# Scores and values of two steps at once in a windowed-attention kernel, with PSUM banks laid out anew

## The chip, the cores and the metric

The kernel runs on one core of a Trainium2 chip. The metric is device time in microseconds (us) for one execution of the whole program. Engines: PE is TensorE's matrix multiplication, PEld its weight load, DVE is VectorE, ACT is ScalarE, POOL is GpSimd, SP issues the transfers.

## The reference, cut to what matters

First comes a selective state-space block (about the first 365 us of the profile, untouched by this change apart from one mask tile). Then come six transformer layers on a batch of 2 sequences of 1,024 rows of width 128, all in fp32. In each layer, 16 heads of 64, windows of 32:

```python
qkv = x @ Wqkv;  q, k, v = split(qkv)
q = rotary(l2norm(q) * qs) * scale;  k = rotary(l2norm(k) * ks) / scale
sim  = einsum('bhwie,bhwje->bhwij', q, look_back(k)) * 8    # 32 queries by 64 keys
attn = softmax(where(mask, -big, sim))
out  = einsum('bhwij,bhwje->bhwie', attn, look_back(v))     # then out @ Wo
# then a layer norm and a gated feed-forward, a * gelu(gate) @ W2
```

## The kernel before

The attention is cut into 384 steps. A step is one pair of heads on 256 rows, 8 windows. A phase is 32 steps: one layer for one sequence, pairs outside, four pieces of rows inside. There are 12 phases. The part of the previous phase that follows the attention (output projection, norm, feed-forward) is threaded into the steps of the phase that runs, at the step numbers `u = n % 32` that the constants `U_WO` (output projection, two halves), `U_MEAN`, `U_DEV`, `U_VAR`, `U_INV`, `U_Z` and `U_FFN` name.

Step `m` is software-pipelined over loop turns `n`. Each engine runs an order written out by hand, once a turn, and semaphores tie the engines together: `then_inc` on the instruction that produces, `wait_ge` ahead of the one that needs. The count a wait asks for is the number of steps that must have got so far. What happens to step `m`:

| work | engine | turn before | semaphore |
|---|---|---|---|
| project q, k (banks 0, 1) and v (bank 5, upper half) | PE L1033, L1040 | m | qk_ps, v_ps |
| squares, and v copied to SBUF | ACT L1266, L1285 | m | sq, v_cp |
| sums of squares (`norms`) | DVE L1385 | m | ss |
| rotary products (`tables`), read from banks 0, 1 | DVE L1404, L1406 | m+1 | prods |
| inverse norms, of two steps at once (`norm_pair`) | ACT L1220, L1223 | every second turn | rn |
| rotary sums, scaling | POOL L1505 to L1510 | m+2 | qk |
| transpose q, k (bank 2), copy | PE L1019, ACT L1259 | m+4 | qkT |
| mask products, scores (banks 3, 4) | PE L975, L981 | m+5 | s_ps |
| row minimum (`least`), exponents | DVE L1361, ACT L1233 | m+5 | mn, pr |
| transpose exponents (bank 6), copy | PE L1054, ACT L1275 | m+6 | pT |
| values (banks 5, 6), reciprocal and scaling (`normalise`) | PE L1000, DVE L1373, L1376 | m+7 | o_ps, on |
| transpose the output (bank 3), copy to OT | PE L958, ACT L1248 | m+8 | oT |

Scores and values use the array in tiles of 64 rows by 32 columns; one step has 32 of each product. All else on PE uses the whole 128 by 128. In fp32 each product of the code is two instructions in the profile. A bank of PSUM that one engine writes is not read by another at the same time: several waits exist only for that, such as the one of the v projection for `on`.

## Time and profile before

| | |
|---|---|
| runs | 2062.97, 2067.97, 2070.41 us; median 2067.97 |
| the profiled execution | 2066.36 us |
| its span in the trace | 2064.6 us (1.8 us lie around it) |
| busy, share of the span | PE 96%, DVE 74%, ACT 67%, POOL 59% |
| mean granted clock of TensorE | 0.978 of full |

Busy time counts an instruction from its start to its end. Neighbours on one engine overlap: a PE product is in flight for some 0.2 us after the next has begun. So what one costs is the distance from its start to the next one's start, and the durations add up to more than that.

### The profile page before, as it was taken

How to read it: one execution, taken by the hardware profiler on the slowest of the kernel's cores; microseconds unless marked ns; L12 is line 12 of the kernel's file. 1: busy time of each engine (PE TensorE's matmuls, PEld its weight loads, DVE VectorE, ACT ScalarE, POOL GpSimd, SP SyncE). 2: the span in 40 equal slices, each digit the busy share in tenths (PEclk: the TensorE clock that was granted, in tenths of full speed). 3: DMA queues.
4: the chain of work that ended last, by engine and by line, in shares of the span. 5: the costliest groups of instructions: out<-in, count | busy, mean ns of one | idle time of the engine just before them, and what ended most of it. 6: DMA issues, size and time to landing. Idle time of an engine off the chain costs nothing.

```text
span 2064.6 us, 82312 instructions
## 1 busy us (share of the span) xinstructions
PE 1989.6 (96%) x33044; PEld 1399.8 (68%) x33044; DVE 1518.1 (74%) x2875; ACT 1383.4 (67%) x4164; POOL 1225.6 (59%) x1374
## 2 busy tenths in 40 slices
PE   7789798999999999999999999999999999999998
PEld 3333233887686786876876877868768778687684
DVE  1499897886796776867867967769678678686783
ACT  4533233886786777767867867768678677776783
POOL 1376774775584565765746855648557567565570
PEclk9888989999999999999999999999999999999999
DMA  1321110311131111121211311112211111111110
GB/s 62 134 72 70 63 61 0 105 44 38 39 90 42 40 43 39 45 77 36 53 37 37 96 38 41 44 32 50 76 47 43 40 39 49 38 43 33 24 40 22
DMA packets 148091, 104.30 MB, mean 51 GB/s; under 512 B 15778, under 2 KB 140256, under 8 KB 146176
## 3 DMA queue, kind: packets, MB, share of 16 engines
q1 hardware_dynamic: 147712, 99.07, 17.3%
q8 instruction: 259, 4.24, 0.9%
q14 instruction: 120, 0.98, 0.1%
HBM read 48.31 MB, written 1.18 MB: 24 GB/s over the span
## 4 chain that ended last, share of the span: by engine, by line
PE 82%; issue 0%; POOL 0%; ACT 0%; DVE 0%; POOLq 0%; ACTq 0%
PE ps L1033 20%; PE ps L1040 9%; PE ps L1019 8%; PE ps L1058 8%; PE ps L1000 8%; PE ps L981 7%; PE ps L1054 4%; PE ps L958 4%; PE ps L1098 3%; PE ps L1092 3%; PE ps L1103 3%; PE ps L975 2%; PE ps L1078 1%; PE ps L1087 1%; PE ps L1133 0%
## 5 line engine op out<-in xcount | busy, mean ns | idle before, releaser
L1510 POOL TENSOR_TENSOR QK<-QK,RN 128x512 f32<-128x512 f32 x384 | 400.8, 1044 | 374.2 <-ACT RN L1223 359.1
L1233 ACT ACTIVATE PR<-ps,MN 128x64 f32<-128x64 f32 x1536 | 357.3, 316 | 154.6 <-DVE MN L1361 139.8
L1033 PE MATMUL ps<-W,XS 128*128 128x256 f32 x1536 | 435.3, 406 | 4.9 <-PEq L64 4.1
L1505 POOL TENSOR_TENSOR QK<-PC,PS 128x256 f32<-128x256 f32 x384 | 280.7, 731 | 246.4 <-PE ps L1019 243.7
L1259 ACT COPY QKT<-ps 128x512 f32<-128x512 f32 x384 | 225.0, 586 | 248.6 <-PE ps L1019 248.6
L1385 DVE TENSOR_REDUCE SS<-SQ 128x8 f32<-128x512 f32 x384 | 262.3, 683 | 58.0 <-ACT SQ L1266 55.2
L1033 PEld LDWEIGHTS ps<-W,XS 128*128 128x128 f32 x1536 | 261.0, 189 | 61.5 <-issue 4.9
L1506 POOL TENSOR_TENSOR QK<-PC,PS 128x256 f32<-128x256 f32 x384 | 281.3, 733 | 0.0
L1361 DVE TENSOR_REDUCE MN<-ps 128x4 f32<-128x256 f32 x384 | 163.0, 424 | 149.8 <-PE ps L981 148.5
L1404 DVE TENSOR_TENSOR PC<-ps,TC 128x512 f32<-128x512 f32 x384 | 261.4, 681 | 0.1
L1406 DVE TENSOR_TENSOR PS<-ps,TS 128x512 f32<-128x512 f32 x384 | 260.7, 679 | 0.0
L1266 ACT ACTIVATE SQ<-ps 128x512 f32<-128x512 f32 x384 | 244.2, 636 | 3.7 <-PE ps L1033 3.7
L1040 PEld LDWEIGHTS ps<-W,XS 128*128 128x128 f32 x1536 | 213.4, 190 | 49.1 <-DVE ON L1376 20.6
L1040 PE MATMUL ps<-W,XS 128*128 128x128 f32 x1536 | 240.2, 279 | 1.2 <-issue 1.2
L1019 PE MATMUL ps<-ident,QK 128*128 128x128 f32 x1536 | 233.8, 273 | 0.9 <-POOL QK L1510 0.6
L1000 PE MATMUL ps<-V,PT 64*32 64x65 f32 x12288 | 227.2, 226 | 0.2
L1019 PEld LDWEIGHTS ps<-ident,QK 128*128 128x128 f32 x1536 | 182.7, 141 | 45.7 <-issue 42.5
L716 POOL TENSOR_TENSOR scr<-U,scr 128x1024 f32<-128x1024 f32 x64 | 150.7, 2355 | 80.8 <-DVE scr L599 80.6
L1000 PEld LDWEIGHTS ps<-V,PT 64*32 64x32 f32 x12288 | 190.6, 105 | 0.9 <-issue 0.8
L484 ACT ACTIVATE ps<-DL,a_neg 128x1024 f32<-128x1024 f32 x64 | 71.6, 1118 | 169.0 <-DVE scr L599 167.7
L981 PE MATMUL ps<-QKT 64*32 64x64 f32 x12288 | 174.5, 222 | 0.0
L1376 DVE TENSOR_TENSOR ON<-ps,RC 128x256 f32<-128x256 f32 x384 | 162.9, 424 | 13.6 <-DVE RC L1373 0.5
(142 smaller groups left out, 3226.7 us busy)
## 6 DMA issues: line engine op xcount, KB each, us to landing
V<-V SPq DMA_DIRECT2D x384, 97.5 KB, 2.2
scr<-B_rows SPq DMA_DIRECT2D x32, 512.0 KB, 3.5
V<-V SPq DMA_DIRECT2D x288, 32.5 KB, 2.4
W<-in_Wqkv SPq DMA_DIRECT2D x40, 192.0 KB, 2.8
TC<-in_tcos SPq DMA_DIRECT2D x6, 1024.0 KB, 5.9
TS<-in_tsin SPq DMA_DIRECT2D x6, 1024.0 KB, 8.5
WO<-in_Wo SPq DMA_DIRECT2D x6, 512.0 KB, 4.1
W<-in_W SPq DMA_DIRECT2D x6, 341.0 KB
```

The costliest lines, as they stand in the source:

```text
L981: mm = nc.tensor.matmul(ps[32 * quad:32 * quad + 32, 3 + h, slot * DH:(slot + 1) * DH], QKT[DH * h:DH * h + DH, 0, c0:c0 + WIN], QKT[DH * ...
L1000: mm = nc.tensor.matmul(ps[32 * quad:32 * quad + 32, 5 + slot, h * (DH + 1):(h + 1) * (DH + 1)], PT[r, m % 2, h, 32 * quad:32 * quad + 32] ...
L1019: mm = nc.tensor.transpose(ps[:, 2, (x * 2 + k) * P:(x * 2 + k + 1) * P], src, ident[:])
L1033: mm = nc.tensor.matmul(ps[:, par, k * 2 * P:(k + 1) * 2 * P], cols[k], W[:, i, 0:2, :].rearrange("p t m -> p (t m)"), start=True, stop=True)
L1040: mm = nc.tensor.matmul(ps[:, 5, (2 + k) * P:(3 + k) * P], cols[k], W[:, i, 2, :], start=True, stop=True)
L1233: e = nc.scalar.activation(PR[:, m % 2, h, slot * DH:(slot + 1) * DH], ps[:, 3 + h, slot * DH:(slot + 1) * DH], ACT.Exp, scale=-1.0, bias= ...
L1385: nc.vector.tensor_reduce(SS[:, p % 2, 8 * k:8 * k + 8], SQ[:, n % 2, :, :], AX.X, ALU.add).then_inc(ss, 1)
L1404: nc.vector.tensor_tensor(PC[:, par, :, :].rearrange("p (k a) d -> p k (a d)", k=2), src, TC[l % 2][:, 2 * s:2 * s + 2, :], ALU.mult)
L1406: nc.vector.tensor_tensor(PS[:, par, :, :].rearrange("p (k a) d -> p k (a d)", k=2), src, TS[l % 2][:, 2 * s:2 * s + 2, :], ALU.mult).then ...
L1505: nc.gpsimd.tensor_tensor(QK[:, par, :, 0:hd], PC[:, par, :, 0:hd], PS[:, par, :, hd:DH], ALU.add)
L1506: nc.gpsimd.tensor_tensor(QK[:, par, :, hd:DH], PC[:, par, :, hd:DH], PS[:, par, :, 0:hd], ALU.add).then_inc(rot, 1)
L1510: nc.gpsimd.tensor_tensor(QK[:, par, :, :], QK[:, par, :, :], bcast_last(RN[:, m // 2 % 2, 8 * par:8 * par + 8], DH), ALU.mult).then_inc(q ...
```

## The change

- **Scores and values.** In every even turn, PE makes the scores of steps n-6 and n-5 together, then the values of steps n-8 and n-7 together; in odd turns neither. A mask product now covers both steps (256 columns instead of 128, from a mask tile with three parts).
- **Row minimum and normalise** run in even turns only, once for two steps: one reduction of 512 elements a partition, one reciprocal of 8, two multiplications. On DVE they now come after `clamp_pair` and `tables`.
- **Banks.** Scores of two steps take the lower halves of banks 3 and 4. The v projection moves from bank 5 to the upper half of bank 4, the transposed output to the upper half of bank 3, the transposed exponents to the last quarters of banks 5 and 6.
- **Waits.** The v projection is now apart from that of q and k (`project_v`), and waits for `pr >= n - 5`: the exponents of the same turn. The second q, k product of an even turn waits for the minimum of the same turn. The transposes of q and k for an odd turn are made in the even turn before it, between the two projections. The exponents of an odd turn wait for the output transposes of that turn, whose second one waits for the v copy of the turn before.
- **ScalarE's order.** `copy_qk`, (`norm_pair` in even turns,) `exponents`, `copy_out`, `squares`, `copy_v`, `copy_p`.
- Later parts of the pipeline shift by a turn (exponents in m+6 or m+5, output transposes m+9), the threaded part by one turn (`U_FFN` 16 to 17), and the loop drains for 9 turns instead of 8.

```diff
-U_WO, U_MEAN, U_DEV, U_VAR, U_INV, U_Z, U_FFN, U_TAB = (6, 8), (7, 9), (8, 10), (10, 12), (11, 13), (12, 14), 16, 17
...
-                return 8 <= n < NSTEPS
+                return 10 <= n < NSTEPS
...
-                m = n - 8
+                m = n - 9
...
+                    if steady(n) and n % 2 == 1 and k == 1:
+                        pe.wait_ge(v_cp, n)
...
                     src = ON[:, m % 2, :, :].rearrange("p (k h) d -> p k (h d)", k=2)[:, k, :]
-                    mm = nc.tensor.transpose(ps[:, 3, (1 + k) * P:(2 + k) * P], src, ident[:])
+                    mm = nc.tensor.transpose(ps[:, 3, (2 + k) * P:(3 + k) * P], src, ident[:])
...
+                if n % 2 or not 0 <= n - 6 < NSTEPS:
+                    return
...
+                    if h == 0:
+                        pe.wait_ge(v_cp, min(n, NSTEPS))
                     if steady(n) and h == 1:
-                        pe.wait_ge(v_sh[(n - 7) % 4], 32 * ((n - 7) // 4 + 1))
-                    nc.tensor.matmul(ps[:, 3 + h, 0:P], identb[:], MASKB[:, int(s == 0), h, :], start=True, stop=True)
+                        pe.wait_ge(v_sh[(n - 8) % 4], 32 * ((n - 8) // 4 + 1))
+                    nc.tensor.matmul(ps[:, 3 + h, 0:2 * P].rearrange("p (f c) -> p f c", f=2), identb[:],
+                                     MASKB[:, f:f + 2, h, :], start=True, stop=True)
                 if steady(n):
...
+                    pe.wait_ge(v_sh[(n - 7) % 4], 32 * ((n - 7) // 4 + 1))
+                for m in (n - 6, n - 5):
+                    s = place(m)[3]
...
+                            mm = nc.tensor.matmul(ps[32 * quad:32 * quad + 32, 3 + h, o0:o0 + DH],
...
+                    mm.then_inc(s_ps, 1)
...
+                if n % 2 or not 0 <= n - 8 < NSTEPS:
                     return
...
+                    for m in (n - 8, n - 7):
...
+                pe.wait_ge(pT, n - 6)
+                for m in (n - 8, n - 7):
+                    for h in range(2):
+                        for slot, quad in spread_tiles:
+                            j = window(slot, quad)
+                            r = slice(64 * slot, 64 * slot + 64)
+                            o0 = (2 * (m % 2) + h) * (DH + 1)
+                            mm = nc.tensor.matmul(ps[32 * quad:32 * quad + 32, 5 + slot, o0:o0 + DH + 1],
...
+                                                  V[r, 2 * (m % 8) + j // 4, 2 * (1 - j % 2) + h, :], start=True, stop=True)
+                    mm.then_inc(o_ps, 1)
...
+                if not steady(n) or n % 2:
                     wait(pe, qkT, m)
                 pe.wait_ge(qk, m + 1)
...
+                        if steady(n) and n % 2 == 0 and (x, k) == (1, 0):
+                            pe.wait_ge(oT, n - 9)
                         src = QK[:, m % 2, :, :].rearrange("p (k x h) d -> p k x (h d)", k=2, x=2)[:, k, x, :]
                         mm = nc.tensor.transpose(ps[:, 2, (x * 2 + k) * P:(x * 2 + k + 1) * P], src, ident[:])
                 mm.then_inc(qkT_ps, 1)
...
                 wait(pe, prods, n - 1)
                 cols = [XS[:, b, PAD + s * STEP + k * P:PAD + s * STEP + (k + 1) * P] for k in range(2)]
                 for k in range(2):
+                    if k == 1 and n % 2 == 0:
+                        wait(pe, mn, n - 4)
                     mm = nc.tensor.matmul(ps[:, par, k * 2 * P:(k + 1) * 2 * P], cols[k],
                                           W[:, i, 0:2, :].rearrange("p t m -> p (t m)"), start=True, stop=True)
                 mm.then_inc(qk_ps, 1)
+
+            def project_v(n):
+                if n >= NSTEPS:
+                    return
...
-                wait(pe, on, n - 6)
+                wait(pe, pr, n - 5)
                 for k in range(2):
-                    mm = nc.tensor.matmul(ps[:, 5, (2 + k) * P:(3 + k) * P], cols[k], W[:, i, 2, :], start=True, stop=True)
+                    if steady(n) and n % 2 == 1 and k == 1:
+                        pe.wait_ge(pT, n - 6)
+                    mm = nc.tensor.matmul(ps[:, 4, (2 + k) * P:(3 + k) * P], cols[k], W[:, i, 2, :], start=True, stop=True)
                 mm.then_inc(v_ps, 1)
...
+                wait(pe, on, min(n - 6 - n % 2, NSTEPS))
                 for h in range(2):
-                    if h == 1 and 7 <= n < NSTEPS - 1:
+                    if h == 1 and n % 2 and 7 <= n < NSTEPS - 1:
                         pe.wait_ge(qkT, n - 3)
-                    mm = nc.tensor.transpose(ps[:, 6, (2 + h) * P:(3 + h) * P], PR[:, m % 2, h, :], ident[:])
+                    if h == 1 and n % 2 == 0 and steady(n + 1):
+                        pe.wait_ge(oT, n - 8)
+                    mm = nc.tensor.transpose(ps[:, 5 + h, 3 * P:4 * P], PR[:, m % 2, h, :], ident[:])
                 mm.then_inc(pT_ps, 1)
...
-                qk_transposed(n)
+                if n % 2 == 0:
+                    qk_transposed(n)
                 out_transposed(n)
                 scores(n)
                 values(n)
                 project(n)
+                if n % 2 == 0:
+                    qk_transposed(n + 1)
+                project_v(n)
                 p_transposed(n)
...
+                p = (n - 2) // 2
+                if n % 2 or not 0 <= p < NSTEPS // 2:
...
-                m = n - 5
+                m = n - 6
...
+                if m % 2:
+                    wait(act, oT_ps, min(n - 8, NSTEPS))
                 for h in range(2):
                     for slot in range(2):
+                        o0 = (m % 2) * P + slot * DH
...
+                                                 ps[:, 3 + h, o0:o0 + DH], ACT.Exp, scale=-1.0,
+                                                 bias=MN[:, h, 2 * (m % 2) + slot:2 * (m % 2) + slot + 1])
                 e.then_inc(pr, 1)
...
+                act.wait_ge(mn, min(n - 4 - n % 2, NSTEPS))
...
+                nc.scalar.copy(PT[:, m % 2, :, :], ps[:, 5:7, 3 * P:4 * P]).then_inc(pT, 1)
...
+                if n % 2 and n >= 9:
+                    act.wait_ge(v_sh[(n - 7) % 4], 32 * ((n - 7) // 4 + 1))
...
-                               ps[:, 5, 2 * P:4 * P].rearrange("p (k a d) -> p k a d", k=2, d=DH)).then_inc(v_cp, 1)
+                               ps[:, 4, 2 * P:4 * P].rearrange("p (k a d) -> p k a d", k=2, d=DH)).then_inc(v_cp, 1)
...
+                if n % 2 == 0:
+                    copy_qk(n)
+                    norm_pair(n)
+                    exponents(n)
+                    copy_out(n)
+                    squares(n)
+                    copy_v(n)
+                    copy_p(n)
+                else:
+                    copy_qk(n)
+                    exponents(n)
                 if u == U_FFN and t >= 0:
                     load_set(nc, act, GELU)
...
                     gates(t, (0,))
+                    copy_v(n)
+                    gates(t, (1,))
                     copy_p(n)
...
                     load_set(nc, act, EXP_LN)
-                else:
+                elif n % 2:
                     copy_out(n)
                     squares(n)
+                    copy_v(n)
                     copy_p(n)
-                    copy_v(n)
...
+                if n % 2 or not 0 <= n - 6 < NSTEPS:
+                    return
+                dve.wait_ge(s_ps, n - 4)
+                wait(dve, pr, n - 6)
+                nc.vector.tensor_reduce(MN[:], ps[:, 3:5, 0:2 * P].rearrange("p h (a d) -> p h a d", d=DH),
+                                        AX.X, ALU.min).then_inc(mn, 2)
...
+                p = (n - 8) // 2
+                if n % 2 or not 0 <= n - 8 < NSTEPS:
+                    return
+                dve.wait_ge(o_ps, 2 * p + 2)
+                o = ps[:, 5:7, 0:4 * (DH + 1)].rearrange("p s (q d) -> p s q d", q=4)
+                wait(dve, on, 2 * p)
+                nc.vector.reciprocal(RC[:].unsqueeze(3), o[:, :, :, DH:DH + 1]).then_inc(rc, 1)
+                dve.wait_ge(rc, p + 1)
+                for k in range(2):
+                    wait(dve, oT_ps, 2 * p + k - 1)
+                    nc.vector.tensor_tensor(ON[:, k, :, :].rearrange("p (s h) d -> p s h d", s=2),
+                                            o[:, :, 2 * k:2 * k + 2, 0:DH], bcast_last(RC[:, :, 2 * k:2 * k + 2], DH),
+                                            ALU.mult).then_inc(on, 1)
...
+                clamp_pair(n)
+                tables(n)
                 least(n)
                 normalise(n)
-                clamp_pair(n)
-                tables(n)
                 norms(n)
```

## Rows read from the trace of the kernel before

**Rows 1.** The page: busy times, and the chain that ended last, by engine.

```profile
PE 1989.6 (96%) x33044; PEld 1399.8 (68%) x33044; DVE 1518.1 (74%) x2875; ACT 1383.4 (67%) x4164; POOL 1225.6 (59%) x1374
...
PE 82%; issue 0%; POOL 0%; ACT 0%; DVE 0%; POOLq 0%; ACTq 0%
```

**Rows 2.** PE in order of start, one step; columns start, duration (both us), instruction.

```profile
1283.88 0.60 PE L1019 MATMUL ps<-ident,QK 128*128 128x128 f32 x4
...
1284.53 0.28 PE L975 MATMUL ps<-MASKB,identb 128*128 128x128 bf16 x2
...
1285.00 0.59 PE L1000 MATMUL ps<-V,PT 64*32 64x65 f32 x32
1285.53 1.13 PE L1033 MATMUL ps<-W,XS 128*128 128x256 f32 x4
1286.49 0.61 PE L1040 MATMUL ps<-W,XS 128*128 128x128 f32 x4
...
1287.16 0.60 PE L1019 MATMUL ps<-ident,QK 128*128 128x128 f32 x4
```

**Rows 3.** PE in narrow windows: where tiled products begin and end.

```profile
1212.82 0.22 PE L975 MATMUL ps<-MASKB,identb 128*128 128x128 bf16 x1
1212.97 0.29 PE L981 MATMUL ps<-QKT 64*32 64x64 f32 x8
...
1213.61 0.22 PE L1000 MATMUL ps<-V,PT 64*32 64x65 f32 x1
1213.76 0.48 PE L1033 MATMUL ps<-W,XS 128*128 128x256 f32 x1
...
1214.08 0.59 PE L1033 MATMUL ps<-W,XS 128*128 128x256 f32 x2
```

**Rows 4.** ACT in order of start, a stretch without gaps.

```profile
1220.07 0.38 ACT L1285 COPY V<-ps 128x256 f32<-128x256 f32 x1
1220.33 0.70 ACT L1295 ACTIVATE DEV<-ps,epsc 128x512 f32<-128x512 f32 x1
1221.06 0.63 ACT L1297 ACTIVATE DEV<-DEV 128x512 f32<-128x512 f32 x1
1221.60 0.57 ACT L1259 COPY QKT<-ps 128x512 f32<-128x512 f32 x1
1222.07 0.93 ACT L1233 ACTIVATE PR<-ps,MN 128x64 f32<-128x64 f32 x4
...
1223.12 0.64 ACT L1266 ACTIVATE SQ<-ps 128x512 f32<-128x512 f32 x1
```

**Rows 5.** DVE in order of start; x2 is two instructions.

```profile
1284.23 0.69 DVE L1385 TENSOR_REDUCE SS<-SQ 128x8 f32<-128x512 f32 x1
...
1286.28 0.68 DVE L1404 TENSOR_TENSOR PC<-ps,TC 128x512 f32<-128x512 f32 x1
1286.88 0.68 DVE L1406 TENSOR_TENSOR PS<-ps,TS 128x512 f32<-128x512 f32 x1
...
1208.04 1.39 DVE L1412 TENSOR_TENSOR XS<-XS,ps 64x512 f32<-64x512 f32 x2 [6.03 <-PE ps L1058]
```

**Rows 6.** What follows a release: four engines in order of start, idle before in brackets.

```profile
1212.75 0.59 ACT L1259 COPY QKT<-ps 128x512 f32<-128x512 f32 x1 [0.60 <-PE ps L1019]
...
1213.55 0.42 DVE L1361 TENSOR_REDUCE MN<-ps 128x4 f32<-128x256 f32 x1 [0.55 <-PE ps L981]
...
1214.17 0.42 DVE L1376 TENSOR_TENSOR ON<-ps,RC 128x256 f32<-128x256 f32 x1
...
1214.64 0.19 PEld L1040 LDWEIGHTS ps<-W,XS 128*128 128x128 f32 x1 [0.16 <-DVE ON L1376]
...
1214.73 0.30 PE L1040 MATMUL ps<-W,XS 128*128 128x128 f32 x1
```

**Rows 7.** Windows in the state-space part: span, busy by engine, granted clock, DMA.

```profile
228.50:259.20 30.70, 24.68 (x54) 9.17 (x53) 28.95 (x18) 9.22 (x9) 27.52 (x19) 1.00 0.18 68
259.20:262.60 3.40, 3.40 (x5) 1.33 (x4) 3.15 (x3) 0.87 (x2) 2.79 (x2) 0.50 0.01 2
```

More of the change, by code:

```diff
@@ L689, in _ @@
             pool.wait_ge(s_id, 1)
-            nc.gpsimd.tensor_copy(MASKB[:].rearrange("p f h c -> p (f h c)"), MASK).then_inc(s_half, 1)
-            nc.gpsimd.tensor_copy(identb[:], ident[:])
+            for f, first in enumerate((1, 0, 0)):
+                nc.gpsimd.tensor_copy(MASKB[:, f, :, :].rearrange("p h c -> p (h c)"), MASK[:, first * 2 * P:(first + 1) * 2 * P])
+            nc.gpsimd.tensor_copy(identb[:], ident[:]).then_inc(s_half, 1)
             pool.wait_ge(ld_qks, 16)
@@ L952, in out_transposed @@
                 if not steady(n):
-                    wait(pe, pr, min(n - 5, NSTEPS))
+                    wait(pe, pr, min(n - 6, NSTEPS))
+                    wait(pe, mn, min(n - 6 + n % 2, NSTEPS))
                     wait(pe, oT, m)
@@ L963, in scores @@
-                if not 0 <= m < NSTEPS:
+                if n % 2 or not 0 <= n - 6 < NSTEPS:
                     return
-                b, l, i, s, par = place(m)
-                if m == 0:
+                if n == 6:
                     pe.wait_ge(s_ones, 2)
                 if not steady(n):
-                    wait(pe, pr, m)
-                    wait(pe, oT, m - 3)
-                    pe.wait_ge(qkT, m + 1)
+                    wait(pe, pr, n - 6)
+                    wait(pe, oT, min(n - 9, NSTEPS))
+                    pe.wait_ge(qkT, n - 4)
@@ L985, in scores @@
-                mm.then_inc(s_ps, 1)
+                    pe.wait_ge(v_sh[(n - 7) % 4], 32 * ((n - 7) // 4 + 1))
+                for m in (n - 6, n - 5):
+                    s = place(m)[3]
+                    for slot in range(2):
+                        for h, quad in spread_tiles:
+                            c0 = PAD + s * STEP + window(slot, quad) * WIN
+                            o0 = (m % 2) * P + slot * DH
+                            mm = nc.tensor.matmul(ps[32 * quad:32 * quad + 32, 3 + h, o0:o0 + DH],
+                                                  QKT[DH * h:DH * h + DH, 0, c0:c0 + WIN],
+                                                  QKT[DH * h:DH * h + DH, 1, c0 - WIN:c0 + WIN],
+                                                  start=False, stop=True, skip_group_check=True)
+                    mm.then_inc(s_ps, 1)
@@ L987, in values @@
             def values(n):
-                m = n - 7
-                if not 0 <= m < NSTEPS:
+                if n % 2 or not 0 <= n - 8 < NSTEPS:
                     return
                 if not steady(n):
-                    pe.wait_ge(pT, m + 1)
-                    pe.wait_ge(v_sh[m % 4], 32 * (m // 4 + 1))
-                    wait(pe, on, m)
-                wait(pe, v_cp, min(n, NSTEPS))
-                for h in range(2):
-                    for slot, quad in spread_tiles:
-                        j = window(slot, quad)
-                        r = slice(64 * slot, 64 * slot + 64)
-                        mm = nc.tensor.matmul(ps[32 * quad:32 * quad + 32, 5 + slot, h * (DH + 1):(h + 1) * (DH + 1)],
-                                              PT[r, m % 2, h, 32 * quad:32 * quad + 32],
-                                              V[r, 2 * (m % 8) + j // 4, 2 * (1 - j % 2) + h, :], start=True, stop=True)
```

66 lines of the change are left out of this document (14 added, 52 removed).

## The prediction

> **What bounds the kernel now.** I read the page first. The chain that ended last is 82% PE, with nothing else above 0%, and PE is busy 96% of the span [rows 1]. So the question became what one step costs on PE and whether it ever waits. PE in order of start answers both [rows 2]: a step takes 1287.16 - 1283.88 = 3.28 us, start to start, without a gap. Most of the 384 steps repeat that number. Per turn, six transposes take 0.65, masks and scores 0.47 (1284.53 to 1285.00), values and the way to the projection 0.53, the q, k projection 0.96, then v projection and two transposes 0.67. Anything that PE does less pays in full, and any new wait of PE costs in full. ScalarE is busy 67% of the span, VectorE 74% [rows 1]; neither sets the pace. Of ScalarE's spacings (start to start, without gaps) [rows 4] gives 0.26 for the copy of v (I take the same for the exponents' copy, of as many elements), 0.47 for the q, k copy, 0.93 from the first exponent to the end of the fourth, 1.05 from the first exponent to the squares.
>
> **What it removes.** PE changes between full and tiled products twice a step. The last mask starts at 1212.82, the first score at 1212.97: 0.15 instead of 0.06. The last value starts at 1213.61, the first projection at 1213.76: 0.15, where its neighbours follow at about 0.01. That first projection needs 0.32 (to 1214.08), where three more in 0.96 - 0.32 make 0.21 each [rows 2, 3]. So one round in and out costs 0.09 + 0.14 + 0.11 = 0.34. Between scores and values another 0.05 goes, an estimate. A pair of steps now has one round instead of two: 0.39 saved. The masks cost the same: two of 256 columns for four of 128 (bounded by 0.06 and 0.11 each; if a wide one cost as little as a narrow one, 0.1 more a pair). PE alone would need 6.56 - 0.39 = 6.17 a pair; times 192 pairs that is 75 us saved.
>
> **What it adds: the frame of a pair on PE**, in us from the first transpose of the even turn, if nothing waits. Output transposes 0.44, masks 0.65, scores 0.96, last score 1.46, values 1.49, last value 2.20, q, k projection 2.35, its second product 2.88, transposes for the odd turn 3.32, v projection 3.75, its last product 4.08, exponent transposes 4.20. Odd turn: output transposes 4.41, q, k projection 4.63, v projection 5.50, exponent transposes 5.94, end 6.17.
>
> Latencies come from [rows 6]. ACT starts 0.31 after the start of PE's last product (one mask and three transposes back from 1212.82, at 0.06 and 0.11, the last q, k transpose starts at 1212.44, and its copy at 1212.75). DVE starts 0.35 after the last score (1213.20 by the 0.27 that scores take, to 1213.55). DVE's product ends at 1214.59, the weight load starts at 1214.64, PE's product at 1214.73: 0.14 from a release to PE. On one engine it is 0.03 (1221.03 to 1221.06) [rows 4].
>
> *Even turn.* The minimum starts at 1.46 + 0.35 = 1.81 if DVE is free. A reduction of 512 is 0.69 [rows 5]; least could cost 0.42, as 256 do now [rows 6], at most twice that, 0.85; I take 0.69. It ends at 2.50, PE may go on at 2.64, before 2.88. The exponents run from 2.53 to 3.46, and 3.60 is before 3.75. Reciprocal and products end by about 3.5, before 4.20; so does the output copy, by about 3.9. All this is covered, with 0.15 to 0.3 to spare.
>
> *Odd turn: here it breaks.* The v copy can't begin before 4.08 + 0.31 = 4.39. ScalarE then has the v copy (0.26), the exponents' copy (0.26), the q, k copy (0.47), and only then the odd step's exponents (0.93), which end at 6.31. `project_v` of the odd turn waits for them, since it writes the bank that they read: 6.31 + 0.14 = 6.45, where PE is ready at 5.50. That is a stall of 0.95 in every pair. Nothing can be in front of it: PE's whole odd projection is already over. Behind the waiting product are queued the exponent transposes and the next pair's scores. The wait for the v copy at the odd output transpose lies inside the same chain (4.39 + 0.38 + 0.14 = 4.91 against 4.52) and costs nothing more.
>
> The row's order on ScalarE is what counts here. The profile shows its instructions only ever in program order. 
> A second chain closes over DVE: odd exponents, 1.05 to the squares, 0.64 for them, 0.03, the sum (0.69), 0.03 and the clamp (0.10, estimated), rotary products 1.20, minimum 0.69, 0.03, exponents 0.93, 0.14, four v products 0.33 to the last, 0.31, copies 0.26 + 0.26 + 0.47: 7.16 a pair. The first gives 6.17 + 0.95 = 7.12. They are as good as equal; I take 7.13, so +0.57 for a pair.
>
> **Pairs with threaded work** (u = 8 to 19), each against before:
> - (8,9), (10,11): the mean's product (2 x 0.43) comes between v_ps and the odd projection and covers 0.86 of 0.95. But the two additions after the output projection (1.39 [rows 5]) now stand, with clamp and rotary products, before the minimum. They start about 0.2 into the turn (an estimate: the last product of the output projection is still in flight): 0.20 + 1.39 + 0.10 + 1.20 = 2.89, ends 3.58, PE goes on at 3.72 instead of 2.88: 0.84, plus 0.07 for the exponents. Before, some 0.13 was lost. Together -0.39 + 0.10 + 0.91 - 0.13 = +0.5 each.
> - (12,13), (14,15): the two activations of the inverse deviation (1220.33 to 1221.60, 1.27 [rows 4]) now end an even row, inside the chain: +0.57 + 1.27, less 0.1 lost before: +1.7 each.
> - (18,19): the additions of the feed-forward (estimated at 1.5 on DVE, by the 1.39 of [rows 5]) stand before the minimum like those above: +0.57 + 1.0 - 0.3 = +1.3.
> - Pair (16,17) holds the feed-forward: its own chain is unchanged, +0.57.
>
> A phase: 11 x 0.57 + 2 x 0.5 + 2 x 1.7 + 1.3 = 12.0. Eleven phases 132, the first (no threaded work) 9, one more turn of draining 1: +142. From the profiled 2066.4 that is 2208; that execution stands 1.6 under the median of the runs, which is less than their spread. I say 2205.
>
> **Bounds.** Low: latencies and overlaps better by 0.1 in each chain (-19), the inverse hidden (-28), minimum 0.42: 2150. High: minimum 0.85, which lengthens the second chain by 0.16 (+31), 0.1 more of latency (+19): 2260. POOL, busy 59% [rows 1], is no bound: its input is ready a turn before its result is needed.
>
> **The rivals.**
> 1. *The saving comes through, faster.* ScalarE's row hides in its own idle time and PE doesn't stand at `project_v`. This decides if the stretch from v_ps to the odd exponents' end is at most 1.42 + 0.39 = 1.81 (equal) or 1.42 (all saved), where I add 0.31 + 0.26 + 0.26 + 0.47 + 0.93 + 0.14 = 2.37. For it: ScalarE is busy 67% of the span and has time to spare [rows 1]. Against it: each term is a row. Time 2066 - 75 = 1991, about 2000 with the stalls of u = 8 to 19.
> 2. *The clock.* TensorE is granted 1.00 (2.4 GHz) all through the attention. It would now be idle nearly 1 us of every 7. In the state-space part, PE busy 24.7 of 30.7 us at 1.00 was followed by 3.4 us at 0.50 (1.2 GHz) [rows 7]. If that came here once in 34 us, each would cost some 1.1 us (half of 3.4, for the two thirds of the pair that PE sets): 48 x 1.1 = 54, so 2260; as often as once in 14 us, 2340. Against it: idle here is 13%, there 20%.
> 3. *DVE becomes the bound* through a wide minimum near 0.85: 2236, within my range.
>
> **Chances.** Forecast with its bounds (rival 3 in it) 0.79; rival 2 0.12; rival 1 0.06; a stall of just about what is saved, 0.03. The range 2145 to 2265 takes in the bounds and the mild end of rival 2. A measurement here can't tell less than 0.3% (6 us) from no change: faster 0.07, same 0.02, slower 0.91.
>
> **What would show it.** Right: PE's biggest idle is before `project_v`, released by ACT's exponents, 0.9 to 1.0 us long, once a pair; score starts 7.1 apart; L1033's first product slow once a pair; a second idle of about 0.8 at u = 8, 10, 18 released by the minimum; 1.2 more at u = 13, 15. Wrong: no idle before `project_v` and 6.2 a pair (rival 1), stretches at 0.50 after 400 us (rival 2), a minimum over 0.8 (rival 3), or a saving that is not 0.39.

## The result, and the profile after

The changed kernel takes 2281.93 us (median of three, 2276.24 to 2282.14) against 2067.97: 1.103 times as long, 95% interval 1.0989 to 1.1072. The forecast was 2205 (2145 to 2265): the direction was right, the time 77 us too short. The profiled execution has a span of 2280.1 us against 2064.6.

From the page, by engine: busy times, the chain that ended last, and two of the costliest groups (busy, mean ns | idle before).

```profile
PE 2034.3 (89%) x32660; PEld 1359.1 (60%) x32660; DVE 1460.2 (64%) x2491; ACT 1426.2 (63%) x4164; POOL 1238.2 (54%) x1376
...
PE 62%; ACT 12%; issue 7%; DVE 3%; ACTq 0%; DVEq 0%
...
L1058 PE MATMUL ps<-W,XS 128*128 128x128 f32 x1536 | 259.3, 291 | 102.1 <-ACT PR L1260 98.3
...
L1010 PE MATMUL ps<-V,PT 64*32 64x65 f32 x12288 | 184.4, 228 | 8.2 <-issue 8.2
```

The chain was 82% PE, with nothing else above 0% [rows 1]. Now it goes through ScalarE for 12%, and 98.3 us of PE's idle time stand before the v projection, released by the exponents: the stall that was forecast, where it was forecast. One ordinary pair on PE, in order of start:

```profile
1445.58 0.60 PE L1027 MATMUL ps<-ident,QK 128*128 128x128 f32 x4
...
1446.23 0.38 PE L980 MATMUL ps<-MASKB,identb 128*128 128x256 bf16 x2
1446.55 0.81 PE L990 MATMUL ps<-QKT 64*32 64x64 f32 x61
...
1448.06 1.13 PE L1043 MATMUL ps<-W,XS 128*128 128x256 f32 x4
1449.03 0.60 PE L1027 MATMUL ps<-ident,QK 128*128 128x128 f32 x4
1449.47 0.61 PE L1058 MATMUL ps<-W,XS 128*128 128x128 f32 x4
...
1450.13 0.74 PE L962 MATMUL ps<-ident,ON 128*128 128x128 f32 x2
1450.71 1.03 PE L1043 MATMUL ps<-W,XS 128*128 128x256 f32 x4
1452.13 0.71 PE L1058 MATMUL ps<-W,XS 128*128 128x128 f32 x4 [0.39 <-ACT PR L1260]
1452.68 0.38 PE L1074 MATMUL ps<-ident,PR 128*128 128x128 f32 x2
1452.89 0.59 PE L1078 MATMUL ps<-OT,WO 128*128 128x512 f32 x1
```

The pair takes 1452.89 - 1445.58 = 7.31, where [rows 2] give 6.56. ScalarE in the same stretch:

```profile
1450.11 0.38 ACT L1313 COPY V<-ps 128x256 f32<-128x256 f32 x1 [0.15 <-PE ps L1058]
1450.38 0.38 ACT L1301 COPY PT<-ps 128x256 f32<-128x256 f32 x1
1450.64 0.60 ACT L1285 COPY QKT<-ps 128x512 f32<-128x512 f32 x1
1451.12 0.95 ACT L1260 ACTIVATE PR<-ps,MN 128x64 f32<-128x64 f32 x4
```

Spacings 0.27, 0.26, 0.48, and the odd v projection 1.01 after the first exponent: the four links of the forecast's first chain, back to back. Its idle is printed as 0.39, not 0.95. Part of the delay is taken earlier: 0.36 at the second output transpose, which waits for the v copy (1450.13 to 1450.71 is 0.58, where the even turn has 0.22). Here it is 0.55: four q, k products that don't follow tiled ones need 0.87, so PE was ready at 1451.58. The printed idle begins only when the last of them is no longer in flight. 0.36 and 0.55 make 0.91, for 0.95 forecast.

Pair by pair (q, k projection to q, k projection, mean over phases 1 to 10), the difference to the kernel before, beside the forecast:

| pairs of a phase | before to after, each | difference | forecast |
|---|---|---|---|
| the eleven forecast at +0.57 | eight of them 6.57 to means of 7.31 to 7.55 (medians 7.30 to 7.34); (4,5) 6.80 to 8.12; (6,7) 14.50 to 14.19, (16,17) 23.70 to 24.15 | +7.8 | +6.3 |
| (8,9), (10,11) | 14.46 to 15.88, 7.48 to 10.12 | +4.1 | +1.0 |
| (12,13), (14,15) | 7.47 to 9.82, 6.92 to 8.55 | +4.0 | +3.4 |
| (18,19) | 6.57 to 8.80 | +2.2 | +1.3 |
| a phase | | +18.1 | +12.0 |

The first two rows are not like for like. The threaded work moved on by one turn, and with it a product for the mean (0.86) went from pair (6,7) to pair (10,11). The forecast left that out. It changes no sum, but with that product taken out of both pairs the first row is +8.7 and the second +3.2.

### The profile page after: what moved, and what is told of

Its sections match the earlier page's. It is cut to its first block, busy times and chain, and to the rows that moved or that the text cites. A ratio compares the mean times of both kernels' runs of the same rounds, so it can differ in the third digit from the quotient of the medians.

```text
span 2280.1 us, 80744 instructions
## 1 busy us (share of the span) xinstructions
PE 2034.3 (89%) x32660; PEld 1359.1 (60%) x32660; DVE 1460.2 (64%) x2491; ACT 1426.2 (63%) x4164; POOL 1238.2 (54%) x1376
## 3 DMA queue, kind: packets, MB, share of 16 engines
q8 instruction: 257, 4.21, 0.8%
## 4 chain that ended last, share of the span: by engine, by line
PE 62%; ACT 12%; issue 7%; DVE 3%; ACTq 0%; DVEq 0%
PE ps L1058 10%; PE ps L1043 9%; PE ps L1027 7%; PE ps L1078 7%; ACT PR L1260 7%; PE ps L990 6%; PE ps L1010 5%; PE ps L1118 3%; PE ps L1112 3%; PE ps L1123 3%; ACT PT L1301 3%; PE ps L1074 2%; PE ps L962 2%; PE ps L980 2%; ACT QKT L1285 2%
## 5 line engine op out<-in xcount | busy, mean ns | idle before, releaser
L1043 PE MATMUL ps<-W,XS 128*128 128x256 f32 x1536 | 427.8, 397 | 44.5 <-DVE MN L1396 37.2
L1058 PE MATMUL ps<-W,XS 128*128 128x128 f32 x1536 | 259.3, 291 | 102.1 <-ACT PR L1260 98.3
L1058 PEld LDWEIGHTS ps<-W,XS 128*128 128x128 f32 x1536 | 203.1, 192 | 180.6 <-ACT PR L1260 171.0
L1027 PEld LDWEIGHTS ps<-ident,QK 128*128 128x128 f32 x1536 | 189.1, 142 | 52.1 <-issue 32.4
L962 PE MATMUL ps<-ident,ON 128*128 128x128 f32 x768 | 183.7, 286 | 22.6
L1010 PE MATMUL ps<-V,PT 64*32 64x65 f32 x12288 | 184.4, 228 | 8.2 <-issue 8.2
L1078 PE MATMUL ps<-OT,WO 128*128 128x512 f32 x384 | 169.9, 593 | 0.0
L1313 ACT COPY V<-ps 128x256 f32<-128x256 f32 x384 | 143.7, 374 | 39.4 <-PE ps L1058 20.9
L990 PE MATMUL ps<-QKT 64*32 64x64 f32 x12288 | 165.2, 224 | 0.0
```

The lines of the kernel that those rows point to most:

```text
L990: mm = nc.tensor.matmul(ps[32 * quad:32 * quad + 32, 3 + h, o0:o0 + DH], QKT[DH * h:DH * h + DH, 0, c0:c0 + WIN], QKT[DH * h:DH * h + DH, ...
L1010: mm = nc.tensor.matmul(ps[32 * quad:32 * quad + 32, 5 + slot, o0:o0 + DH + 1], PT[r, m % 2, h, 32 * quad:32 * quad + 32], V[r, 2 * (m % 8 ...
L1027: mm = nc.tensor.transpose(ps[:, 2, (x * 2 + k) * P:(x * 2 + k + 1) * P], src, ident[:])
L1043: mm = nc.tensor.matmul(ps[:, par, k * 2 * P:(k + 1) * 2 * P], cols[k], W[:, i, 0:2, :].rearrange("p t m -> p (t m)"), start=True, stop=True)
L1058: mm = nc.tensor.matmul(ps[:, 4, (2 + k) * P:(3 + k) * P], cols[k], W[:, i, 2, :], start=True, stop=True)
L1078: mm = nc.tensor.matmul(ps[:, wo_bank(t, c), :], WO[:, k, :], OT[:, c, k, :], start=(k == 0), stop=(k == PAIRS - 1), skip_group_check=True)
```

## The experiments

All start from the changed kernel unless another is named. The ratio is to the kernel before, run on the same chip; "pair" is the median of the eight pairs of a phase without threaded work, phases 1 to 10.

| run | us | ratio (95%) | pair |
|---|---|---|---|
| e1_copy_in_chain | 2347.17 | 1.134 (1.131 to 1.137) | 7.62 |
| e2_copy_in_idle | 2279.79 | 1.102 (1.098 to 1.105) | 7.32 |
| e3_minimum_first | 2482.30 | 1.200 (1.197 to 1.203) | 8.64 |
| e4_exps_first_min_first | 2436.29 | 1.178 (1.175 to 1.182) | 8.38 |
| f5_clamp_min_first | 2242.07 | 1.084 (1.082 to 1.087) | 7.32 |
| f6_exps_first | 2285.97 | 1.105 (1.102 to 1.108) | 7.58 |
| f7_exps_and_min_first | 2214.78 | 1.071 (1.069 to 1.074) | 7.06 |
| f8_all_three | 2231.76 | 1.079 (1.078 to 1.081) | 7.31 |
| g1_inverse_odd | 2271.85 | 1.099 (1.097 to 1.101) | 7.31 |
| g2_inverse_odd_clamp_min | 2229.62 | 1.079 (1.077 to 1.081) | 7.32 |
| g3_three_edits | 2202.75 | 1.066 (1.064 to 1.069) | 7.07 |
| g4_both_exponents_even | 2141.24 | 1.036 (1.034 to 1.038) | 6.74 |
| h1_split_changed | 2318.35 | 1.121 (1.119 to 1.122) | 7.58 |
| h2_split_both_exponents | 2129.00 | 1.029 (1.026 to 1.032) | 6.74 |
| h3_var_later_both_exponents | 2124.63 | 1.028 (1.026 to 1.031) | 6.75 |
| h4_var_later_inverse_odd | 2251.47 | 1.088 (1.086 to 1.090) | 7.32 |

**Is it the chain through ScalarE?** One more copy (256 elements a partition, into a tile that nobody reads) in even rows, once inside the chain and once in ScalarE's idle time before the even exponents.

```diff
+            def extra():
+                nc.scalar.copy(JNK[:], XRES[:, 0:STEP])
...
                     copy_p(n)
+                    if 10 <= n < NSTEPS:
+                        extra()
```

In e2 the same two lines stand behind `norm_pair(n)` instead.

> The changed kernel with one more ScalarE copy (128x256, SBUF to SBUF, result unused) at the end of each even row from turn 10 on, that is between the exponents' copy and the odd row. Theory A (a chain from the even turn's v projection through ScalarE's copies and the odd exponents to the odd v projection sets the pair): the copy's 0.26 us comes on top in every one of some 187 pairs, +50 us, about 2332 us, and TensorE's wait before the odd v projection grows by 0.26. Theory B (a chain over VectorE's sums and minimum, or TensorE's own work, sets the pair, and the wait is slack): 0 to +10 us.

> The same extra copy, but after norm_pair in each even row, where ScalarE in the profile waits 1.0 us for the minimum. Theory A: nothing, 2282 us within 6 us. Theory C (ScalarE's total work sets the pair, wherever it stands): +50 us, as in the kernel with the copy in the chain.

The same work costs 65 us in one place and nothing (-2) in the other. Pair 7.62 against 7.32. What counts is the place in ScalarE's row and not its load: the chain is shown. (e1 came out 15 us above its forecast. Its pair grew by 0.30 instead of 0.26, some 7 us in 187 pairs, and its clock fell more often, which is told below and can hold the rest.)

**What may VectorE's order do?** The minimum ahead of clamp and rotary products; then behind the clamp only.

```diff
-                clamp_pair(n)
-                tables(n)
                 least(n)
                 normalise(n)
+                clamp_pair(n)
+                tables(n)
                 norms(n)
```

This is e3. In f5 `clamp_pair(n)` stays first and `tables(n)` alone moves.

> The changed kernel with VectorE's old order in even turns: least, normalise, clamp_pair, tables, norms. Theory A: the ordinary pair stays at 7.30 us (7.25 to 7.35), since the chain over ScalarE is untouched; the pairs at u = 8, 10 and 18, where TensorE now waits 1.1 us for a minimum that stands behind additions and rotary products, lose that wait: 3 x 1.1 x 11 = 36 us, about 2246 us. Theory B (the chain over VectorE sets the ordinary pair): the pair falls below 7.2 us, and the gain is over 50 us.

> As the kernel with the minimum first, which came out 200 us slower, but with the clamp kept ahead of it: clamp_pair, least, normalise, tables, norms. In that kernel ScalarE's norm_pair, which stands before the exponents in its row, waited 478 us in all for a clamp that had moved behind the minimum and normalise. If that was the cause, it is gone here: the ordinary pair is 7.30 us again (7.25 to 7.40), and the pairs at u = 8, 10 and 18 lose their wait for the minimum: 36 us, about 2246 us. If the order itself hurts (rotary products late), the ordinary pair is above 7.5.

e3 missed badly, on the other side of its forecast. Its chain of waits names the reason in one line (total us, times, longest):

```profile
ACT SS L1244 <- DVE SS L1427: 478.3, 192, 4.7
```

`norm_pair` stands ahead of the even exponents on ScalarE and needs the clamp; with the clamp behind the minimum and both products of `normalise`, every pair pays. In the changed kernel the same wait is 35.1 us in all. I had costed the wait that I removed and not the one that the moved instruction carries. f5 keeps the clamp in front and lands where forecast: 2242, with u = 8 from 15.9 to 14.7, u = 10 from 10.1 to 8.9, u = 18 from 8.8 to 7.6, and the ordinary pair unchanged. That is the second term of the forecast (the minimum late at u = 8, 10, 18), shown and worth 40 us.

**The chain without the q, k copy.** In odd rows the exponents come ahead of `copy_qk`; the wait for the v copy moves from the odd output transpose to the odd v projection, so that it doesn't close a circle.

```diff
                 else:
-                    copy_qk(n)
                     exponents(n)
+                    copy_qk(n)
...
-                    if steady(n) and n % 2 == 1 and k == 1:
-                        pe.wait_ge(v_cp, n)
...
+                if steady(n) and n % 2:
+                    pe.wait_ge(v_cp, n)
```

> The changed kernel, VectorE's order untouched; in odd rows the exponents go before the q, k copy, and the wait for the v copy moves from the second output transpose to the odd v projection. The chain over the copies gets 0.47 shorter, the one over VectorE (odd squares, sum, clamp, rotary products, minimum, exponents, v projection, v copy) stays as long as it is, 0.13 below the pair of now. With both chains real, the ordinary pair is 7.17 us and the time 2257 us (2245 to 2265). If VectorE's chain doesn't bind, 6.83 and 2194 us.

> As the kernel with the minimum first, and besides: in odd rows the exponents go before the q, k copy, and the wait for the v copy moves from the second output transpose to the odd v projection, so that the exponents need not wait for it. Theory A: the chain gets 0.47 us shorter and the ordinary pair 7.30 - 0.47 = 6.83 us; with the 36 us of the order, 2282 - 88 - 36 = 2160 us (2145 to 2185). Theory B: the squares of the odd step come 0.47 later, which lengthens the chain over VectorE unless its order is the old one, as here; then no more than the 36 us, 2246 us. A third possibility is that the rotary products, now late in even turns, make TensorE wait at the odd q, k projection: 6.9 to 7.1 us a pair.

> Both edits: exponents first in odd rows, and clamp, minimum, normalise ahead of the rotary products. Both chains are shorter: the ordinary pair 6.83 us, unless TensorE waits at the odd q, k projection for the rotary products that are now late (ready at about 5.2 us of the pair, where the projection is due at 4.6), which gives 6.85 to 6.95. Time 2246 - 88 = 2158 us (2145 to 2180). If neither chain is the cause, nothing beyond the 36 us.

Alone (f6) it gives nothing (2286 us, for 2257 forecast): the second chain, over VectorE, takes over. ScalarE and VectorE of f6:

```profile
1431.15 0.95 ACT L1260 ACTIVATE PR<-ps,MN 128x64 f32<-128x64 f32 x4
...
1438.57 0.94 ACT L1260 ACTIVATE PR<-ps,MN 128x64 f32<-128x64 f32 x4
```

```profile
1434.10 0.38 DVE L1427 TENSOR_SCALAR SS<-SS 128x16 f32<-128x16 f32 x1
1434.40 0.68 DVE L1439 TENSOR_TENSOR PC<-ps,TC 128x512 f32<-128x512 f32 x1
```

From odd exponents to odd exponents are 7.42, and each link of the second chain follows the one before it there. In the changed kernel the same circle is 7.18: it has only 0.13 of slack in 7.31, at the even v projection (exponents ready at 1448.27 + 0.93 + 0.14 = 1449.34, product at 1449.47). In f6 the clamp takes 0.30 of it where it took 0.08 (1446.27 to 1446.35), and no run tells why. e4, with e3's order, has e3's wait (479.0 us). With f5's order (f7) the median pair goes to 7.06 and the time to 2215, where 2158 was forecast. So two chains did stand side by side, and undoing one of them shows only the other. Of the 0.47 that leave the first, 0.26 arrive in the median pair; some pairs take 7.7, and the idle inside the values' products (below) grows from 8.2 to 27.3 us.

**The inverse deviation.**

```diff
-U_WO, U_MEAN, U_DEV, U_VAR, U_INV, U_Z, U_FFN, U_TAB = (7, 9), (8, 10), (9, 11), (11, 13), (12, 14), (13, 15), 17, 17
+U_WO, U_MEAN, U_DEV, U_VAR, U_INV, U_Z, U_FFN, U_TAB = (7, 9), (8, 10), (9, 11), (11, 13), (13, 15), (14, 16), 19, 17
```

> The changed kernel with one thing moved: the two activations of the inverse deviation stand in odd turns (u = 13, 15) instead of even ones (12, 14), the steps behind them one or two turns later. Theory A (the chain v projection, ScalarE's copies, odd exponents, odd v projection is what sets a pair; what stands at the end of ScalarE's even row is inside it, what ends the odd row is not): the pairs u = 12 and 14 lose 1.27 each, 11 phases x 2 x 1.27 = 28 us, so 2254. Rival B (ScalarE's work as a sum sets the pair, wherever it stands): no change, 2282.

> The inverse deviation in odd turns as in the run before it, together with VectorE's order clamp, minimum, normalise, tables (that alone gave 2242). Theory A: the two gains touch different pairs' stalls and add up: 2242 - 28 = 2214. Rival B: pairs u = 12 and 14 are then held by VectorE, and only half comes: 2228.

> VectorE's order clamp, minimum, normalise, tables; in odd turns the exponents ahead of the q, k copy; and the inverse deviation in odd turns (the first two alone gave 2215). Theory A: 2215 - 28 = 2187. Rival B (the inverse now delays the odd row of ScalarE, whose v copy the next masks wait for): 2215 or above.

> Exponents first, clamp and minimum first, plus the exponents' copy of the even turn after the odd exponents (chain 0.26 shorter), plus the inverse deviation at the end of odd rows (u = 13, 15, feed-forward at 19) instead of even ones. The last takes 1.27 us each out of two pairs a phase: 28 us. The copy gives nothing if the rotary products bind (6.85 a pair), up to 0.26 if not (6.6): 2130 us by the one, 2080 by the other.

10 us in g1 instead of 28, 12 in g2 and in g3. The pair of u = 14 fell from 8.55 to 7.31, all of 1.24; that of u = 12 only from a mean of 9.8 to 9.5 (its median rose from 9.32 to 9.51). g2 came to its rival's number, 2228, but not by its cause: the pair of u = 14 is 7.31 there too, so VectorE doesn't hold it. PE and ScalarE of g1 there:

```profile
1488.61 0.38 PE L1074 MATMUL ps<-ident,PR 128*128 128x128 f32 x2
1490.19 1.10 PE L1107 MATMUL ps<-DEV,ones 128*128 128x512 f32 x2 [1.20 <-ACT DEV L1323]
1491.12 0.60 PE L1027 MATMUL ps<-ident,QK 128*128 128x128 f32 x4
```

```profile
1489.34 0.70 ACT L1323 ACTIVATE DEV<-ps,epsc 128x512 f32<-128x512 f32 x1
1490.08 0.63 ACT L1325 ACTIVATE DEV<-DEV 128x512 f32<-128x512 f32 x1
```

The second variance product (u = 13) writes bank 7, which the first logarithm reads, now at the end of row 13. It waits 1.20 and the next pair waits behind it. To see whether this is all of it, that product went one turn on, `U_VAR = (11, 14)`:

> The same move of the second variance product in the changed kernel with the inverse deviation in odd turns (2272). Theory A: 13 less, 2259, and the pair from u = 12 falls from 9.5 to 8.3 or less. Rival B: 2272.

2251.47: another 20 us, for 13 forecast, u = 12 at 7.30. Not all of the 30 us together is the inverse: h4 also moves 0.86 of PE work into pair (14,15), where 0.5 of it hides in a stall (7.65, not 7.31 + 0.86), some 6 us in eleven phases. That leaves some 24 us for moving two activations of 1.27 in each phase, near the forecast's 28, and g1 had found another wait. f8 also put the exponents' copy (`copy_p`) behind the odd exponents. It went to 2232 instead of 2130: ScalarE's odd row then ends so late that the next masks wait for its v copy, a chain that I hadn't drawn.

**What is the joined run of tiled products worth?** h1 puts the first q, k product of the even turn between scores and values and leaves all else.

```diff
                 scores(n)
+                project(n, (0,))
                 values(n)
-                project(n)
+                project(n, (1,))
```

> The changed kernel, with the first q, k product of the even turn put between scores and values, so that a pair has two runs of 64 tiled products again instead of one of 128, and all else (banks, waits, two steps at once) stays. Theory A (the joined run saved 0.27 a pair, by the trace of the changed kernel, and every pair pays its TensorE time in full in front of the v projection): pair 7.30 + 0.27 = 7.57, 192 x 0.27 = +52, less the 8 us of idle inside the values' products if these come from the long run: 2326. Theory B (the saving was 0.39 as forecast, and something else made the pair longer): +75 - 8, 2349. Rival C (the joined run saved nothing or is hidden): 2274 to 2282.

```profile
1470.34 0.38 PE L980 MATMUL ps<-MASKB,identb 128*128 128x256 bf16 x2
1470.65 0.86 PE L990 MATMUL ps<-QKT 64*32 64x64 f32 x64
1471.44 0.70 PE L1044 MATMUL ps<-W,XS 128*128 128x256 f32 x2
1472.07 0.86 PE L1010 MATMUL ps<-V,PT 64*32 64x65 f32 x64
1472.86 0.70 PE L1044 MATMUL ps<-W,XS 128*128 128x256 f32 x2
1473.40 0.60 PE L1027 MATMUL ps<-ident,QK 128*128 128x128 f32 x4
```

Masks to the transposes behind the projection: 3.06 here, 1449.03 - 1446.23 = 2.80 in the changed kernel. The pair goes from 7.31 to 7.58. So the round that the change removes is worth 0.27, the ordinary pair pays it in full, and the 0.39 of the forecast was too much. (The time grew by 36 us and not by 44: the pairs at u = 8, 10 and 18 didn't get longer.) The rows of the changed kernel say the same: 7.31 less the waits (0.36 and 0.55) and less 0.11 that a v product loses after its wait is 6.29, and 6.56 - 0.27 is 6.29.

**The order that takes the chain out.** g4 makes the exponents of both steps in the even row, right behind `norm_pair`; ScalarE's odd row holds copies and squares alone, the v copy ahead of the squares. On PE, transposes and the first q, k product of the odd turn go ahead of the even v projection, which waits for both exponents (`pr >= n - 4`; the odd one for `v_cp >= n` alone). VectorE's order is clamp, minimum, tables, normalise; the inverse deviation stands as in g1.

```diff
-                project(n)
                 if n % 2 == 0:
+                    project(n)
                     qk_transposed(n + 1)
-                project_v(n)
-                p_transposed(n)
+                    project(n + 1, (0,))
+                    project_v(n)
+                    p_transposed(n)
+                    project(n + 1, (1,))
+                else:
+                    project_v(n)
+                    p_transposed(n)
```

> The even turn takes the exponents of both steps, right after the inverse norms, instead of one step's in each turn. So the odd v projection no longer waits for ScalarE's odd row, and the chain v projection, copies, odd exponents, odd v projection is gone; the even v projection waits for both exponents instead, and is moved behind the transposes and the first q, k product of the next turn, which cover that wait. VectorE: clamp, minimum, tables, normalise. Inverse deviation in odd turns. Theory A (the pair's length came from that one chain): by the measured durations the minimum ends at 2.5 after the pair's start, eight exponents at 4.5, the even v projection goes at 4.6, the rest of PE's work takes to 6.5: a pair of 6.5 (6.4 to 6.7) against 7.30, 192 x 0.8 = 154 less than 2282 and the inverse, so 2100 (2070 to 2140), about as the kernel before. Rival B (the layout itself costs: whoever writes bank 4 waits for the exponents, and a pair can't do better than the changed kernel with its edits): 2190 or more. Rival C (only the saving of 0.27 a pair counts and nothing else waits): 2066 - 52 = 2015.

> The kernel with both exponents in the even turn (2141), with the second variance product one turn later (u = 14 instead of 13), so that it doesn't stand behind the first inverse deviation. Theory A (that product waited 1.2 once a phase, with the next pair queued behind it): 11 x 1.2 = 13 less, 2128. Rival B (the wait was already hidden, or another takes its place): 2141.

2141: just past theory A's range, 141 us under the changed kernel. g4 holds three edits at once; against g2, which has the inverse and nearly VectorE's order of g4, the new order of the exponents and of PE is worth 88. An undisturbed pair takes 6.56 (1452.25 to 1458.81 between scores), others more, so that the eight mean 6.9. The new layout itself costs little, against rival B. With the variance product moved (h3) it is 2125, still 1.028 times the kernel before. No version here reaches the kernel before; what the last 57 us are made of wasn't taken apart, beyond 25.7 us of the idle that comes next.

**Idle inside the values' products.** PE idle by releaser, in g4 and then in h2, which is g4 with h1's split:

```profile
PE ps L1010 <- issue: 28.4, 33, 2.0
```

```profile
PE ps L1010 <- issue: 6.3, 13, 1.7
```

> The same split in the kernel with both steps' exponents in the even turn (2141). There TensorE alone needs 6.29 of a pair of 6.56, so the 0.27 of the split should be covered for the most part (at most 0.05 a pair left, 10 us). Theory A (the idle inside the values' products, 28 us in that kernel, comes because one long run of tiled products uses instructions up faster than the queue fetches them): that idle falls to a few us, and the time to 2113 to 2123. Rival B (the idle has to do with something else, such as transfers of the weights at that time): it stays, 2141 to 2151. Rival C (the idle goes, but the split is paid in full): 2141 - 28 + 52 = 2165.

22 of the 28 us go when the run of 128 tiled products becomes two of 64, and the time falls by 12 though PE has 0.27 more to do in each pair. 2129 is above theory A's 2113 to 2123 and below both rivals. In the changed kernel the same idle (8.2 us, 9 times) is absent in h1. What it looks like, in the changed kernel:

```profile
1958.75 0.73 PE L1010 MATMUL ps<-V,PT 64*32 64x65 f32 x51
1961.12 0.33 PE L1010 MATMUL ps<-V,PT 64*32 64x65 f32 x11 [1.64 <-issue]
```

51 values' products, 1.64 idle with nothing to wait for, then the rest. The page lists the queue that brings instructions:

```profile
q8 instruction: 257, 4.21, 0.8%
```

257 packets for 4.21 MB are 16 KB each. If they are PE's alone, its 65,320 instructions are 254 a packet, an estimate. A pair's run has 128 products with 128 weight loads, 256: a packet's worth in 1.4 us, where the changed kernel's packets begin 6.9 us apart (median between 800 and 1900 us). In the trace of g4 each of these idles ends 2.2 to 3.2 us after such a packet began. That the engine has run out of instructions is therefore likely. Shown is only that it helps to break the run.

## Why the prediction was wrong in its size

**The mechanism was right.** PE's largest idle is before `project_v`, released by the exponents, once a pair; e1 and e2 show that ScalarE's row between v projection and odd exponents sets the pair, and f6 that a chain over VectorE stands close behind (7.18 by the rows of the changed kernel, 7.16 forecast). The time missed because terms of the sum were mis-sized or missing, and one overlap was wrong. Rival 1 is out: from the last v product (the fourth from 1449.47, at 0.11, so 1449.80) to the odd v projection at 1452.13 are 2.33, for 2.37 forecast. Rival 3 is out: the wide minimum took 0.68, as estimated.

**Term "0.39 saved": mis-sized, 0.27** (h1). It lies in front of the v projection, so each 0.01 of it counts. The joined run is slower than its parts: its 128 products take 1.37 from first to last start (1446.545 to 1447.915), two of 64 in h1 take 0.64 each, 1.29. That is 0.09 of the 0.12. The v copy then starts at +4.53, not +4.39.

**A term that was missing: +0.11.** A v projection that has waited needs 0.55 to the next instruction (1452.13 to 1452.68), one that hasn't 0.44. It is the first of the four products that takes 0.21 instead of 0.11. Its weight load had to wait with it (171.0 us of idle on PEld before this line); that this is the cause is argued, not tested. With the chain's 2.33 for 2.37, 7.12 + 0.12 + 0.11 - 0.04 = 7.31: +0.75 instead of +0.57, 0.18 in each ordinary pair, 1.4 a phase for eight of them.

**Pairs (8,9) and (10,11): +3.2 (without the product that moved) instead of +1.0, the largest error of any pair.** VectorE and PE at u = 8, PE and ScalarE at u = 9:

```profile
1459.96 1.39 DVE L1447 TENSOR_TENSOR XS<-XS,ps 64x512 f32<-64x512 f32 x2 [6.41 <-PE ps L1078]
1461.38 0.58 DVE L1427 TENSOR_SCALAR SS<-SS 128x16 f32<-128x16 f32 x1
1461.99 0.69 DVE L1439 TENSOR_TENSOR PC<-ps,TC 128x512 f32<-128x512 f32 x1
...
1463.19 0.68 DVE L1396 TENSOR_REDUCE MN<-ps 128x8 f32<-128x512 f32 x1
```

```profile
1463.93 0.70 PE L1043 MATMUL ps<-W,XS 128*128 128x256 f32 x2 [1.08 <-DVE MN L1396]
...
1465.65 1.02 PE L1098 MATMUL ps<-XS,ones 128*128 128x512 f32 x2
1466.52 0.38 PE L962 MATMUL ps<-ident,ON 128*128 128x128 f32 x2
...
1468.00 0.71 PE L1058 MATMUL ps<-W,XS 128*128 128x128 f32 x4 [0.23 <-ACT PR L1260]
```

```profile
1466.17 0.61 ACT L1285 COPY QKT<-ps 128x512 f32<-128x512 f32 x1
1467.02 0.93 ACT L1260 ACTIVATE PR<-ps,MN 128x64 f32<-128x64 f32 x4 [0.24 <-PE ps L962]
```

Two steps failed. The minimum began 3.43 after the turn, not 2.89: the clamp took 0.61 behind the additions instead of the estimated 0.10. And the mean's product was said to cover 0.86 of the stall and leave 0.09. 0.40 were left: four q, k products from 1466.73 are done at 1467.60, and the v projection begins at 1468.00. The product covered only half, for the odd exponents wait for the odd output transposes, and these are queued on PE behind the mean: ScalarE waited for them until 1467.02, when its q, k copy (1466.17, 0.48) had been done for 0.37. (18,19) has the late minimum too (1.08 idle at 1531.75, and 8.80 for 7.9 forecast).

**(12,13), (14,15): +4.0 for +3.4**, near; by the medians it is +3.5, for three of the ten (12,13) pairs hold a fall of the clock, 1.7 each. The inverse was worth some 24 us for 28.

**Rival 2, the clock, came in small.** All of the attention ran at 1.00 before. Here TensorE was granted 0.50 (1.2 GHz) in five stretches, 20.4 us in all, each at the end of an unusual idle or right behind it. Two of them, windows before, in and after (PE busy is the first number after the span, the clock the third from the end):

```profile
645.90:649.30 3.40, 0.90 (x7) 0.72 (x6) 2.32 (x5) 1.26 (x5) 2.42 (x4) 1.00 0.94 368
649.30:652.70 3.40, 2.97 (x11) 2.53 (x11) 0.00 (x0) 1.87 (x7) 0.17 (x1) 0.50 0.10 28
652.70:656.10 3.40, 3.40 (x144) 2.93 (x142) 2.29 (x4) 2.75 (x8) 1.56 (x3) 1.00 0.20 51
```

```profile
1171.50:1174.90 3.40, 1.63 (x9) 1.17 (x9) 1.54 (x3) 3.37 (x11) 3.08 (x4) 1.00 0.14 34
1174.90:1178.30 3.40, 3.40 (x12) 2.26 (x11) 2.06 (x4) 1.03 (x3) 0.00 (x0) 0.50 0.16 39
```

At half speed they cost at most half of their length, 10 us. Three of the five stand behind the 1.63 stall of pair (12,13); the ordinary stall of a pair never brought one. e1 had fifteen such stretches, 54.6 us in all. Rival 2 as stated (one in 34 us, or in 14) is out. (Its 48 x 1.1 is 53, not 54; nothing hangs on it.)

**The rest.** Pair (4,5) has a mean of 8.12: 8.24 to 10.95 in phases 2, 4, 6 and 8, in which the tables come in, and 7.2 to 7.6 in the others. The 10.95 is the first window above: 2.92 us in which PE, with no wait, had nothing to run, while the tables' 2 MB came in at a DMA share of 0.94:

```profile
646.20 0.60 PE L1027 MATMUL ps<-ident,QK 128*128 128x128 f32 x4
649.73 0.59 PE L1058 MATMUL ps<-W,XS 128*128 128x128 f32 x2 [2.92 <-issue]
```

The page counts the tables' transfers among the DMA issues (KB each, us to landing):

```profile
TC<-in_tcos SPq DMA_DIRECT2D x6, 1024.0 KB, 5.0
TS<-in_tsin SPq DMA_DIRECT2D x6, 1024.0 KB, 8.5
```

After the packet at 637.63 the instruction queue began no other until 647.41, and the idle (from 646.80) ended 2.32 us after that one, as the idles inside the values' products do. That instructions stood behind those transfers is therefore likely, but not tested.

By the table, with the moved product taken out, the miss in a phase is 2.4 + 2.2 + 0.6 + 0.9 = 6.1, so 61 us in phases 1 to 10. Phase 0 (99.8 to 112.6, 9 forecast) and phase 11 (136.7 to 152.5, 12 forecast) add 3.8 each, the drain behind the last projection (61.9 to 69.2, 1 forecast) 6.3, and the part before the attention was 1.3 shorter: 74, the distance from 2208 to the profiled execution of 2281.9.

## What to carry to other kernels

When two steps' work is joined, draw the whole circle of each engine's row before counting what the join saves: here it saved 0.27 us a pair and made a circle (v projection, three ScalarE instructions, exponents, v projection) that cost 1.0. What took most of that away was the order of ScalarE's row and the place of the waiting product, not less work. Work threaded into such a circle covers the stall only as far as nothing of the circle is queued behind it on its engine: the mean's product of 0.86 hid 0.5. And moving an instruction moves its own waits: e3, g1 and f8 each gave back part of their gain, or more, to a wait that the moved instruction carried or that others had on it.

## What the runs showed of the hardware

- Of a run of tiled products the first 32 or so (with as many weight loads) start about 7.5 ns apart, later ones about 12 on average: before the change 32 scores took 0.24 (1284.737 to 1284.976), the 32 values behind them 0.38. So a joined run has one fast start where two runs have two, which is where it loses 0.09. The Trainium skill ("TensorE: Matmul & The Clock Gate", Step-by-step: what each phase is for) tells of a window of 64 instructions in which weight loads are pulled ahead; 32 products with their loads would fill it, but no run here tests that it is the cause.
- Inside a run of 128 tiled products with 128 weight loads PE stood idle for 0.3 to 2 us with no releaser: 28 us in g4, 6 when the run is halved; and once 2.92 us beside a large transfer. Late delivery of instructions is the likely cause, not shown.
- The clamp of 16 elements took 0.58 behind the additions of L1447 and 0.17 in ordinary turns of the same program (0.38 in ordinary turns of f6); no run tells why.
